# Causal attention without mask products: VectorE masks while it takes maxima, GpSimd selects after the exponential, head groups in pairs share one output bank

## The reference

```python
def _L0_attn_ref(x, w_qkv, w_out, head_scales, head_dirs):      # B, T, C, H = 2, 1024, 128, 16; HD = 8
    qkv = (x @ w_qkv).reshape(Bx, Tx, 3, H, HD)
...
    scores = jnp.einsum('bhqd,bhkd->bhqk', q, k) * SCALE
    causal = jnp.tril(jnp.ones((Tx, Tx), dtype=bool))
    scores = jnp.where(causal[None, None], scores, -jnp.inf)
...
    geo_bias = q_proj[..., :, None] * k_proj[..., None, :]
    scores = scores + head_scales[None, :, None, None] * geo_bias
    attn = jax.nn.softmax(scores, axis=-1)
    out = jnp.einsum('bhqk,bhkd->bhqd', attn, v)
    out = jnp.transpose(out, (0, 2, 1, 3)).reshape(Bx, Tx, Cx)
    return out @ w_out
...
x = x + _layernorm(_L0_attn_ref(_layernorm(x, axis=-1), ...), axis=-1)
x = x + _layernorm(_L0_ffn_ref(_layernorm(x, axis=-1), ...), axis=-1)     # mixture of 7 experts, 2 per token, and a shared one
```

## Time and profile before

| what | value |
|---|---|
| time without profile, median of 3 runs | 524.5 us (523.02 to 527.57) |
| span of the profiled execution | 542.4 us |
| PE busy | 440.5 us, 81% of the span |
| DVE busy | 329.6 us, 61% |
| ACT busy | 244.3 us, 45% |
| POOL busy | 142.2 us, 26% |
| mean granted clock of PE | 0.899 of full speed |

### The profile page before, as it was taken

The page is one execution under the profiler, slowest core; times in us unless marked ns, Lnnn a source line. Parts: engine busy times, 40 slices in busy tenths (PEclk is TensorE's granted clock), DMA queues, the critical chain, the costliest instruction groups (busy, mean ns, idle before and its releaser), DMA issues. The chain is left out here.

```text
span 542.4 us, 10816 instructions
## 1 busy us (share of the span) xinstructions
PE 440.5 (81%) x3980; PEld 267.0 (49%) x3980; DVE 329.6 (61%) x885; ACT 244.3 (45%) x432; POOL 142.2 (26%) x211
## 2 busy tenths in 40 slices
PE   1845978989898998999898968888699989898800
PEld 0522432434434352434434345645499889888800
DVE  3975956868787876878782764599223322223356
ACT  1520145666665765677675827552122222213330
POOL 9300000010111101011111002424626665573423
PEclk9975576999989997999988988999979999999965
DMA  3065254100202020000000008100447768766352
GB/s 102 21 179 150 78 157 119 58 5 3 60 2 61 2 60 2 2 3 3 3 2 2 1 2 232 39 2 1 160 137 228 205 194 215 215 206 190 98 160 78
DMA packets 44616, 46.60 MB, mean 86 GB/s; under 512 B 6355, under 2 KB 33364, under 8 KB 44564
## 3 DMA queue, kind: packets, MB, share of 16 engines
q1 hardware_dynamic: 42132, 40.92, 25.8%
q0 software_dynamic: 2432, 4.99, 3.6%
HBM read 34.80 MB, written 10.88 MB: 84 GB/s over the span
## 5 line engine op out<-in xcount | busy, mean ns | idle before, releaser
L611 ACT ACTIVATE probs<-banks 128x1024 f32<-128x1024 f32 (+1 forms) x192 | 145.3, 810 | 80.6 <-PE banks L468 52.5
L749 DVE TENSOR_REDUCE mx_part<-banks 128x1 f32<-128x512 f32 (+3 forms) x256 | 133.2, 584 | 42.1 <-PE banks L444 34.2
L444 PE MATMUL banks<-k_st,q_st 48*128 48x512 bf16 (+3 forms) x384 | 123.9, 370 | 14.5 <-DMA k_st<-k_rows 12.3
L461 PE MATMUL banks<-q_st,k_st 51*128 51x512 bf16 (+3 forms) x384 | 103.7, 349 | 17.7 <-DMA q_st<-mx_rows 11.3
L480 PE MATMUL banks<-probs,v_pad 128*32 128x512 f32 (+3 forms) x768 | 86.8, 526 | 0.0
L461 PEld LDWEIGHTS banks<-q_st,k_st 51*128 51x128 bf16 x384 | 32.1, 96 | 75.7 <-ACT probs L611 49.9
L749 DVE TENSOR_REDUCE mx<-banks 128x1 f32<-128x512 f32 (+3 forms) x128 | 54.7, 485 | 20.1 <-PE banks L450 20.0
L1488 DVE TENSOR_TENSOR hidden<-banks,gate 128x512 f32<-128x512 f32 x38 | 26.3, 692 | 61.6 <-ACT gate L1256 28.8
L355 POOL TENSOR_TENSOR mx_rest<-mx_neg,mx_rows 16x128 f32<-16x128 f32 x16 | 6.7, 417 | 199.2 <-ACT mx_neg L621 199.2
L444 PEld LDWEIGHTS banks<-k_st,q_st 48*128 48x128 bf16 x384 | 34.7, 95 | 43.6 <-DVE mx_part L749 24.8
L448 PE MATMUL banks<-mask_qk,ident_half 64*128 64x128 bf16 x256 | 56.2, 232 | 0.0
(11 more groups left out here) (198 smaller groups left out, 616.1 us busy)
## 6 DMA issues: line engine op xcount, KB each, us to landing
w_g<-in_w_gate SPq DMA_DIRECT2D x38, 256.0 KB
w_u<-in_w_up SPq DMA_DIRECT2D x38, 256.0 KB
q_rows<-parts SPq DMA_DIRECT2D x24, 128.0 KB, 2.4
k_rows<-parts SPq DMA_DIRECT2D x24, 128.0 KB, 2.4
q_st<-q_rows SPq DMA_DIRECT2D x32, 96.0 KB, 2.3
k_st<-k_rows SPq DMA_DIRECT2D x32, 96.0 KB, 2.3
w_d<-in_w_down SPq DMA_DIRECT2D x8, 256.0 KB, 4.9
back<-results SPq DMA_DIRECT2D x8, 256.0 KB, 4.8
```

The costliest lines, as they stand in the source:

```text
L444: last = nc.tensor.matmul(dst[:, 0:width], q_st[r][rows, c, p, (i % CH) * P:(i % CH + 1) * P], k_st[r][rows, kc, p, 0:width], start=True, ...
L461: last = nc.tensor.matmul(dst[a][:, 0:width], k_st[r][rows, j // CH, p, (j % CH) * P:(j % CH + 1) * P], q_st[r][rows, c, p, first:BANK], s ...
L611: nc.scalar.activation(probs[unit % PROBS][:, 2 * p:2 * p + 2, first:BANK], slot_pair[k % 2].rearrange("p (a t) -> p a t", a=2)[:, :, 0:BA ...
L749: nc.vector.tensor_reduce(dst, max_bank[m % RING][:, 0:width], AX.X, ALU.max, negate=True).then_inc(max_taken, 1)
```

## The change

1. **No mask matmuls.** Lines 448, 450, 466 and 468 go, with their tiles `ident_half`, `mask_qk` and `mask_kq`; two matmuls after each of 512 products, 1024 in all.
2. **Maxima.** A masked block (diagonal) is read by one `tensor_tensor_reduce` on DVE instead of `tensor_reduce`. It adds a mask tile from SBUF, negates, writes the masked block to a scratch tile, and takes the minimum down to one column, starting from the off-diagonal result where there is one, so `merge_maxima` goes. Off-diagonal blocks keep `tensor_reduce`.
3. **Scores.** They aren't masked before the exponential; POOL sets the part above the diagonal to zero in `probs` afterwards, one `affine_select` on 4 x 128 columns per diagonal unit, and `weighted_values` of such a unit waits for it (`selected`).
4. **Order.** Groups go in pairs: chunk 0 of the even group, chunk 0 of the odd one, chunk 1 of the even one, chunk 1 of the odd one: a list of 96 units. Maxima run LEAD = 12 units ahead of the scores in this list.
5. **Output bank.** Both groups of a pair add into the same bank, the odd group 16 columns further in each head's 32 columns of `v_pad`; `take_sums`, `turn_outputs` and `take_outputs` come 8 times in place of 16.
6. **Rows.** POOL splits the maxima before PE turns them (`split_rows` now in front of `turn_maxima`), so one bf16 matmul turns all three parts and one ACT copy takes them; `send_rows` still has six DMAs. The turn is at step `CHUNK_LAST + 2 - LEAD`.
7. **Exponentials.** Units 256 and 128 wide fill one slot instead of two and have one ACT instruction.
8. **Start.** SP loads the stacks of group 1's first chunk before it stores the second half of batch 0, and stores half of batch 1 ahead of the first `send_rows`. v is copied by 32 ACT instructions instead of 16.

```diff
+LEAD = 12
+CHUNKS_IN_ORDER = [(2 * g + i, c) for g in range(PAIRS) for c in range(NC) for i in range(2)]
+UNIT_LIST = [(n, x) for n, c in CHUNKS_IN_ORDER for x in range(*CHUNK_X[c])]
+CHUNK_FIRST = [UNIT_AT[n, CHUNK_X[c][0]] for n, c in CHUNKS_IN_ORDER]
+CHUNK_LAST = [UNIT_AT[n, CHUNK_X[c][1] - 1] for n, c in CHUNKS_IN_ORDER]
+TURN_STEP = {CHUNK_LAST[s] + 2 - LEAD: s for s in range(len(CHUNKS_IN_ORDER))}
+SPLIT_STEP = {CHUNK_LAST[s] + 1 - LEAD: s for s in range(len(CHUNKS_IN_ORDER))}
...
+            load_stacks(1, 0)
             store_parts(0, 1)
             load_stacks(0, 1)
-            load_stacks(1, 0)
             load_stacks(1, 1)
-            send_rows(0, 0)
-            for half in range(2):
-                store_parts(1, half)
-            send_rows(0, 1)
+            store_parts(1, 0)
+            send_rows(0)
+            store_parts(1, 1)
+            send_rows(1)
...
+            def select(k):
+                n, x = UNIT_LIST[k]
+                first = SCORE_UNITS[x][2]
+                block_at = probs[k % PROBS][:, :, first:first + P]
+                pool.wait_ge(slot_taken, SLOT_AT["score", k, fills(x) - 1] + 1)
+                nc.gpsimd.affine_select(out=block_at, in_=block_at, compare_op=ALU.is_ge, fill=0.0, base=0,
+                                        pattern=[[0, HG], [1, P]], channel_multiplier=-1).then_inc(selected, 1)
...
+                nc.tensor.matmul(max_bank[m % RING][:, 0:width], q_st[r][rows, c, p, (i % CH) * P:(i % CH + 1) * P],
+                                 k_st[r][rows, kc, p, 0:width], start=True, stop=True).then_inc(max_filled, 1)
...
+            def weighted_values(k):
...
+                pe.wait_ge(slot_taken, SLOT_AT["score", k, fills(x) - 1] + 1)
+                if is_diagonal(x):
+                    pe.wait_ge(selected, DIAGONALS[k])
...
+            def turn_maxima(s):
+                dst = free_slot(("rows", s))
+                pe.wait_ge(rows_split, s + 1)
+                nc.tensor.matmul(dst[0][0:PARTS * HG * CH, 0:P],
+                                 mx_split[s % 2][:, :, :].rearrange("p i j -> p (i j)"), ident_b[:, :],
+                                 start=True, stop=True).then_inc(slot_filled, 1)
...
+            for k in range(STEPS):
+                n, x = UNIT_LIST[k]
+                for p in range(PAIRS_G):
+                    if p < fills(x):
+                        dst = free_slot(("score", k, p))
+                    score(k, p, 0, dst)
+                    if k + LEAD < STEPS:
+                        maxima(k + LEAD, p, 1, 2 * p)
+                    last = score(k, p, 1, dst)
...
+                    if k + LEAD < STEPS:
+                        maxima(k + LEAD, p, 0, 2 * p + 1)
+                if k > 0:
+                    weighted_values(k - 1)
+                if k in TURN_STEP:
+                    turn_maxima(TURN_STEP[k])
...
+                if kc == c:
+                    first = 3.0e38
+                    if c > 0:
+                        first = mx_part[n % 2][:, at:at + 1]
+                        dve.wait_ge(max_taken, HG * (UNIT_AT[n, i] + 1))
+                    nc.vector.tensor_tensor_reduce(masked[m % RING][:, 0:width], src, mask[:, BANK - width:], -1.0, first,
+                                                   ALU.add, ALU.min, mx[c][n % 2][:, at:at + 1]
+                                                   ).then_inc(max_taken, 1)
+                else:
+                    nc.vector.tensor_reduce(mx_part[n % 2][:, at:at + 1], src, AX.X, ALU.max, negate=True
+                                            ).then_inc(max_taken, 1)
```

More of the change, by code:

```diff
@@ L64 @@
 LOADS = 4
+LEAD = 12
+PARTS = 3
 class Count:
@@ L375, in _ @@
[L375 to L384 removed]
+            pool.wait_ge(consts_ready, 1)
+            pool.wait_ge(ones_ready, STACKS)
+            nc.gpsimd.memset(mask[:, 0:BANK - P], 0.0).then_inc(consts_ready, 1)
@@ L387, in _ @@
+            steps = 6 + 4 * NG
+            for k in range(min(SPLIT_STEP), STEPS):
+                if k in SPLIT_STEP:
+                    split_rows(SPLIT_STEP[k], steps + 3 * SPLIT_STEP[k])
+                if k >= 0 and is_diagonal(UNIT_LIST[k][1]):
+                    select(k)
+                if k in INVERT_STEP:
+                    normalise(INVERT_STEP[k])
+            for k in sorted(INVERT_STEP):
+                if k >= STEPS:
+                    normalise(INVERT_STEP[k])
         @block.tensor
@@ L443, in maxima @@
                     pe.wait_ge(max_taken, m - RING + 1)
-                last = nc.tensor.matmul(dst[:, 0:width], q_st[r][rows, c, p, (i % CH) * P:(i % CH + 1) * P],
-                                        k_st[r][rows, kc, p, 0:width], start=True, stop=diagonal is None)
-                if diagonal is not None:
-                    half = slice(a * HALF, (a + 1) * HALF)
-                    nc.tensor.matmul(dst[:, diagonal:width], ident_half[half, 0, :], mask_qk[half, 0, :],
-                                     start=False, stop=False)
-                    last = nc.tensor.matmul(dst[:, diagonal + HALF:width], ident_half[half, 1, :],
-                                            mask_qk[half, 1, HALF:], start=False, stop=True)
@@ L459, in score @@
                 if p == 0 and a == 0 and x in (0, CH):
-                    pe.wait_ge(rows_ready[c], 16 * 6 * (n + 1))
-                last = nc.tensor.matmul(dst[a][:, 0:width],
+                    pe.wait_ge(rows_ready[c][n % 2], 16 * 2 * PARTS * (n // 2 + 1))
+                return nc.tensor.matmul(dst[a][:, at:at + width],
                                         k_st[r][rows, j // CH, p, (j % CH) * P:(j % CH + 1) * P],
-                                        q_st[r][rows, c, p, first:BANK], start=True, stop=not diagonal)
@@ L464, in score @@
-                if diagonal:
-                    half = slice(a * HALF, (a + 1) * HALF)
-                    nc.tensor.matmul(dst[a][:, 0:P], ident_half[half, 1, :], mask_kq[half, 1, :],
-                                     start=False, stop=False)
-                    last = nc.tensor.matmul(dst[a][:, 0:HALF], ident_half[half, 0, :], mask_kq[half, 0, 0:HALF],
-                                            start=False, stop=True)
-                return last
-            def weighted_values(n, x):
-                c, j, first = SCORE_UNITS[x]
-                unit = n * UNITS + x
-                pe.wait_ge(slot_taken, SLOT_AT["score", n, x, PAIRS_G - 1] + 1)
-                if x in (0, CH) and unit > 0:
-                    pe.wait_ge(o_taken, n * NC + c)
+                                        q_st[r][rows, c, p, first:BANK], start=True, stop=True)
@@ new lines, in _ @@
+            for k in sorted(TURN_STEP):
+                if k < 0:
+                    take_rows(TURN_STEP[k])
+            for k in range(STEPS):
+                for p in range(fills(UNIT_LIST[k][1])):
+                    exponentials(k, p)
+                if k in SUMS_STEP:
+                    take_sums(SUMS_STEP[k])
+                if k in TURN_STEP:
+                    take_rows(TURN_STEP[k])
+                if k in OUT_STEP:
+                    take_outputs(OUT_STEP[k])
+            take_sums(len(OUT_LIST) - 1)
```

396 lines of the change are left out of this document (185 added, 211 removed).

## The result

The changed kernel took 534.4 us (median of 4 runs, 529.7 to 537.9) against 523.8 us (518.9 to 527.6, also 4) for the kernel before: a ratio of 1.019, 95% interval 1.012 to 1.026. It is slower, by about 10 us. The profiled execution of after took 533.2 us, with a span of 531.5. The long third part of the first profile of before, 227.5 us against 208.7 in a second one (first experiment), has nothing to do with attention.

What follows compares the result with a forecast made beforehand. PE and DVE were taken to hold each other up through the ring of three banks. Pairs 56.3 + 4.9 + 2.0 = 63.2 us against 61.3 gave +6.6, start -1.6: 524.5 + 5.0 = 529.5 us, range 512 to 546.

Steps and rivals of the forecast that it cites:

- work at full clock: Attention, a pair of groups: 24 steps, turns of rows and outputs at full clock, 56.3 us with e = 0.07.
- waits for rows: PE at second chunks: waits of 3.2 us (odd group) and 1.7 (even), 4.9 a pair against about 2 before.
- low clock: PE behind waits for rows: units at lower granted clock cost 2.0 us a pair, against about 1.3 before.
- e = 0.07: DVE's masked pass: a `tensor_tensor_reduce` costs 0.07 us beyond the `tensor_reduce` it replaces; range 0 to 0.13.
- 54.7 + 23e: A pair's full-clock time: 54.7 us plus 23 times the masked pass's extra cost e on DVE.
- Rivals 2 and 4: Rival 2: DVE becomes the bound, 541 us, chance 0.15. Rival 4: a 1.14 us select on POOL, 540 us, chance 0.08.
- a clock under 0.9 over whole pairs: Sign of failure: the prediction fails if the granted clock of whole pairs falls under 0.9.
- rival 3: Steps 4 to 7 and 20 to 23: PE's narrow work runs at the lower clock, +36 us, 565 us, chance 0.05.
- Rival 1: Rows come in time and the masked pass is nearly free: 7 to 12 us faster, 515 us, chance 0.25.
- +1.9 for each full pair: Attention: a pair takes 63.2 us against 61.3, +1.9; three and a half pairs give +6.6.
- The start: Before attention: first rows are in at 66 us and PE starts there, not at about 67.7: -1.6 us.
- the wait for the second rows: Start of attention: second rows, behind the second store, are in at 79 us, wanted at 74: a 5 us wait.

Runs made afterwards that it cites:

- first experiment: The kernel before, unchanged, run again for a second profile: 529.2 us, span 527.4.
- e2: The changed kernel with the rows of a chunk sent by two DMAs instead of six: 512.7 us, ratio to before 0.975.
- e5: The changed kernel with rows sent by two DMAs and a plain `tensor_reduce` in place of the masked pass: 501.3 us beside 524.0 for before.
- e10: The changed kernel with LEAD = 16 and two small matmuls of zeros behind each masked product: 507.8 us, ratio to before 0.972.
- e9: The kernel before, in its own order, without its 1,024 mask matmuls and nothing in their place: 522.4 us, ratio 0.998.
- e4: The changed kernel with LEAD = 16 and all six DMAs kept: 509.9 us, ratio to before 0.968.
- e3: The changed kernel, six DMAs, with two small matmuls of zeros put back behind each masked product: 532.3 us, ratio to before 1.010.
- e7: The changed kernel with rows sent by two DMAs and matmuls of zeros behind every diagonal product: 505.7 us, ratio to before 0.969.
- e8: The changed kernel with rows sent by two DMAs and LEAD = 14: 520.3 us, median of 11 runs.

## Why the prediction was right, and where not

The forecast was 529.5 us, slower by 5.0 with the new wait for rows as its reason; measured was 534.4, slower by about 10. The sign stands, and so does the place of the new wait. That the number came near is partly luck: the term for the waits was too large and the one for the clock too small. For the mean of the two middle pairs:

| term, us a pair | predicted | measured in after | before, first profile |
|---|---|---|---|
| work at full clock | 56.3 | 56.4 | 58.2 |
| waits for rows | 4.9 | 2.7 | 2.0 |
| low clock | 2.0 | 6.3 (what is left) | 1.4 |
| pair | 63.2 | 65.4 | 61.6 |

Against before the pairs have 1.8 us less work, 0.7 more of waits and 4.9 more of the clock. By work and waits alone these pairs would have been faster; it is the clock that made them slower.

*Work*: the pairs of e2, which have no waits, less 0.25 for each of their 4.6 and 5.7 us at the low clock: 56.9 and 55.9. The 24 steps of a pair, each taken where it ran at full clock in one of e2's two, add up to 56.3. Before, with its waits (2.0) and clock (1.4) taken off in the same manner, had 58.2 in its first profile. So the new order and the removed products did save 1.8 us a pair.

*The masked pass*: e = 0.07 was about right. Without it a pair took 54.7 (e5); the prediction had 54.7 + 23e, and 56.4 gives e = 0.07. Rivals 2 and 4 are out: PE's matmuls waited 4.1 us for the pass in the whole program (its weight loads 40.5, mostly while matmuls still ran: PE was idle for 26.1 us of attention in all, 17.1 of them for the rows), and 0.8 for the select, which took 0.64 us where 0.75 was assumed.

*The rows*: the place and which wait is the longer (odd chunks long, even ones short) were right. The length was 2.3 to 2.5 and 0.8 to 1.0, not 3.2 and 1.7: from the first issue to the released score it took 5.15 us, not 6.0 as in the earlier trace rows, and from the turn to the first issue 0.56, not 0.75.

*The clock* is the step that failed. The prediction took windows of the size of the earlier trace rows behind waits, about one a pair before, and raised them from 1.3 to 2.0 us a pair for the longer waits. In the two pairs 24 and 33 us ran at the low level. Taking 56.4 and the waits (2.3 and 3.1) off 64.1 and 66.7 leaves 5.4 and 7.2 us; at e10's price of 0.25 they would be 6.1 and 8.3. The prediction named a clock under 0.9 over whole pairs as what would prove it wrong, and that is what came. It is near to rival 3, at under half its price (4.3 us a pair more than forecast, 15 in all, against its 36), but not in its place: of the 58 us at the low level in these two pairs 16 lie in the steps 4 to 7 and 20 to 23 that it named. The ground against that rival, that unmasked units run at full clock before, was true of units among masked ones; in e9, without the masks, 62 us ran at the low level where before has 36 and 48, so the masks were part of what kept them so.

*Rival 1* had 515 us if the rows come in time. With the waits taken out, e2 and e4 measured 512.7 and 509.9.

*The sum*: against before's first profile the pairs differ by -2.6, +2.9, +4.8 and +2.5 us, where the prediction had +1.9 for each full pair, and the first score comes 1.8 us earlier: +5.8 in all. Here too errors cancel. The start was forecast as 66 against 67.7 and is 65.2 against 67.0, and the wait for the second rows, expected at 5 us much as in before, was 1.1, one reason why the first pair got shorter. The timed difference is some 4 us more than 5.8, and against before's second profile attention ends only 2 us later. Single profiled executions of before differ by that much, so this rest is not placed.

*What is shown and what not.* Shown: without the waits the same change is 2.5 to 3.2% faster than before (e2, e4). Shown: PE work that computes nothing raises the clock, with waits (e3: 0.88 to 0.89 against 0.83 to 0.85) and without (e7: 0.92 to 0.93 against 0.85 to 0.91; e10: 0.91 to 0.92 against 0.87 to 0.88), and the removal of the mask products lowers it (e9: 0.87 to 0.89 against 0.89 to 0.91). Not shown: that the waits cause the low clock one by one; four stretches began without one, and e4 and e8 have low clock without any. Not explained: why one and the same program (two sends, or 14 ahead) is granted different clocks from run to run. Sending before's rows in two DMAs wasn't tried; their layout there would have to change. So how much of e2's gain before could have had is open; it had 11 us of such waits, about 5 of them in the first group.

## What to carry to other kernels

When a list of work is reordered, measure for each transfer the way from its last input to its first use, and how much work of the new order lies between: here PE stood still for 2.3 us behind two narrow units in each pair, and two DMAs in place of six, or four steps more of lead, turned the change from 2% slower into 3% faster. Before counting on matmuls that are removed, look at the granted clock of the stretch: a thousand of them taken away alone left the time the same (ratio 0.998), as the clock fell from 0.90 to 0.87 in the median. Where the clock differs from run to run, compare runs at equal clocks, and spreads as well as medians.

## What the runs showed of the hardware

- In after a `tensor_tensor_reduce` to one column was two instructions, 688 ns at 512 columns and 83 ns (mean of all widths); the second started together with the next pass, and passes came every 0.61 us. With a start value from a tile the first took 59 ns more (747 against 688).
- Six DMAs of 2 KB took SP 3.97 us to issue in after, two of 6 KB 1.44 us in e2.
- An `affine_select` on 512 columns took 636 ns on POOL in after, on 128 columns 284.
- In e4 the granted clock fell to its low level 2 us behind a stretch of 12.8 us in which PE stood idle for 1.3 (steps 0 to 4); with zeros that left it idle for 0.6 of 13.0 us there (e10) it stayed up.
- A microsecond at the low level cost 0.25 us here (e4 against e10, and 0.26 between runs of e2).
